# Layer 0 scan: one scan instruction for both halves of the channels, with initial states written by TensorE

## The reference

```
A = -jnp.exp(A_logs).reshape(K, d, N)            # K = 4 directions, d = 256, N = 16

def step(h, inp):
    dt_l, u_l, B_l, C_l = inp
    dA = jnp.exp(dt_l[..., None] * A)
    h = h * dA + (dt_l * u_l)[..., None] * B_l[:, :, None, :]
    y = jnp.einsum('bkdn,bkn->bkd', h, C_l)
    return (h, y)
h0 = jnp.zeros((B, K, d, N), x.dtype)            # B = 4 images
_, ys = lax.scan(step, h0, (dt_t, u_t, B_t, C_t))
```

## Time and profile before

| | us |
|---|---|
| median of 3 runs | 9207.98 (9200.64 to 9214.95) |
| profiled execution | 9207.24 |
| its span | 9205.4 |
| four passes of the scan, together | 3414.7 |

### The profile page before, as it was taken

The page is one execution under the profiler, slowest core; times in us unless marked ns, Lnnn a source line. Parts: engine busy times, 40 slices in busy tenths (PEclk is TensorE's granted clock), DMA queues, the critical chain, the costliest instruction groups (busy, mean ns, idle before and its releaser), DMA issues. The chain is left out here.

```text
span 9205.4 us, 142734 instructions
## 1 busy us (share of the span) xinstructions
PE 7794.9 (85%) x50982; PEld 6018.6 (65%) x50982; DVE 5517.8 (60%) x8186; ACT 3754.6 (41%) x7820; POOL 3974.0 (43%) x2456
## 2 busy tenths in 40 slices
PE   8999799989999899953355556688879999999999
PEld 6888588867887688841355553345656666666666
DVE  7999799979999799952233335556662222222222
ACT  6787488747876588720011112203431111111111
POOL 5888388847887488820488880031000000000000
PEclk9999999999999999975677778789999999999999
DMA  2333133312332133322455550000002222222221
GB/s 65 91 91 88 50 91 91 89 58 81 90 90 80 58 90 91 88 100 66 117 159 157 157 158 21 3 0 2 0 7 95 92 86 82 76 99 92 86 92 71
DMA packets 461971, 736.07 MB, mean 80 GB/s; under 512 B 46319, under 2 KB 366984, under 8 KB 459569
## 3 DMA queue, kind: packets, MB, share of 16 engines
q1 hardware_dynamic: 409649, 560.19, 19.4%
q0 software_dynamic: 51840, 169.91, 6.3%
HBM read 707.51 MB, written 43.72 MB: 82 GB/s over the span
## 5 line engine op out<-in xcount | busy, mean ns | idle before, releaser
L591 POOL TENSOR_TENSOR l_arena<-l_arena 128x768 f32<-128x768 f32 x1536 | 2778.6, 1824 | 470.6 <-DVE l_arena L541 408.5
L541 DVE TENSOR_TENSOR_SCAN l_arena<-l_arena,psum 128x384 f32<-128x384 f32 x3072 | 2867.9, 984 | 77.0 <-PE psum L382 41.7
L475 ACT ACTIVATE l_arena<-l_arena,l_A 128x384 f32<-128x384 f32 x3072 | 1665.3, 604 | 81.7 <-DVE l_arena L541 81.6
L384 PE MATMUL psum<-l_arena 128*128 128x128 f32 x11520 | 1579.8, 284 | 28.8 <-DVE l_arena L541 25.1
L384 PEld LDWEIGHTS psum<-l_arena 128*128 128x128 f32 x11520 | 1405.7, 192 | 185.4 <-issue 114.6
L395 PE MATMUL psum<-l_ident,l_arena 128*128 128x128 f32 x9216 | 1259.7, 273 | 53.1 <-ACT l_yT L481 45.5
L1963 DVE TENSOR_TENSOR st_Uc<-psum,st_both 128x384 f32<-128x384 f32 x512 | 285.5, 558 | 1699.8 <-PE psum L1884 1699.8
L976 POOL DMA_INDIRECT l_G<-neighbourhoods,l_idc x648 | 879.6, 1357 | 699.6 <-issue 690.4
L395 PEld LDWEIGHTS psum<-l_ident,l_arena 128*128 128x128 f32 x9216 | 1053.5, 141 | 64.3 <-POOL l_arena L591 41.5
L1884 PE MATMUL psum<-st_F,st_xt 128*128 128x384 f16 (+2 forms) x6912 | 1002.1, 290 | 0.0
L995 PE MATMUL psum<-l_ident,l_G 128*128 128x128 f32 x2592 | 450.2, 356 | 534.9 <-DVE l_G L959 534.9
(11 more groups left out here) (326 smaller groups left out, 7729.2 us busy)
## 6 DMA issues: line engine op xcount, KB each, us to landing
l_arena<-c_rows SPq DMA_DIRECT2D x1536, 192.0 KB, 3.0
st_FS<-filter_sums SPq DMA_DIRECT2D x128, 641.0 KB, 7.4
st_F<-filter_parts SPq DMA_DIRECT2D x128, 576.5 KB, 6.1
neighbourhoods<-padded_image SPq DMA_DIRECT2D x16, 1300.5 KB
st_mab<-in_st_mp SPq DMA_DIRECT2D x68, 256.0 KB, 7.4
st_mab<-in_st_mm SPq DMA_DIRECT2D x68, 256.0 KB, 7.7
l_G<-neighbourhoods,l_idc POOLq DMA_INDIRECT x648, 3.6
l_gnx<-in_x SPq DMA_DIRECT2D x4, 1152.0 KB, 5.6
```

The source lines that it names most:

```text
L384: mm = pe.matmul(ps[:, o:o + P], dtuT[:, g % 2, t, h * P:(h + 1) * P], diagB[:, rank[s] % 3, t, :], start=True, stop=True)
L475: act.activation(decay[:, s % NDC, h, :], dtv[:, g % 2, h, :], ACT.Exp, scale=A[:, g // NRC, h, n:n + 1]).then_inc(s_exp, 1)
L541: dve.tensor_tensor_scan(hbuf[:, n, h, flip], decay[:, s % NDC, h, flip], ps[:, BANK * (2 * (s % 2) + h):BANK * (2 * (s % 2) + h) + RC][:, ...
L591: pool.tensor_tensor(hC[:, s % NHC], hbuf[:, s % NS], Cs[:, s % NCS, :].unsqueeze(1).broadcast_to([P, 2, RC]), ALU.mult).then_inc(s_hc, 1)
```

## The change

`hbuf` and `decay` get rows of `RX` = 772 columns in place of 768: column 0, the 384 positions of half 0, column 385, the 384 of half 1, column 770, and one spare. The decays at columns 0, 385 and 770 are set to zero once a pass. One scan instruction goes over 770 columns, 0 to 769 forward or 770 to 1 backward, from the constant 0. Where the decay is zero the state becomes the scan's input, so TensorE writes each half's initial state into that column of PSUM: a matmul with `ident` as weights and one column of `hbuf` (or of zeros) as moving data, ahead of the half's three blocks. The PSUM set is laid so that half 0 with its column ends a bank and half 1 begins the next. `s_x2` and `s_scan` now count once a step, so waits on a half become waits on a step.

```diff
+RX = 2 * RC + 4
+X2_AT = BANK - RC - 2
...
-        hbuf = cut(0, NS * 2 * RC).rearrange("p (n h l) -> p n h l", n=NS, h=2)
+        hbuf = cut(0, NS * RX).rearrange("p (n l) -> p n l", n=NS)
...
-        decay = cut(20352, NDC * 2 * RC).rearrange("p (r h l) -> p r h l", r=NDC, h=2)
+        decay = cut(20416, NDC * RX).rearrange("p (r l) -> p r l", r=NDC)
...
+                x2_ps = [ps[:, 2 * BANK * r + X2_AT:2 * BANK * (r + 1)] for r in range(2)]
+
+                def half(h):
+
+                    return slice(1 + h * (RC + 1), 1 + h * (RC + 1) + RC)
+
+                def halves(row):
+
+                    return row[:, 1:2 * RC + 3].rearrange("p (h l) -> p h l", h=2)[:, :, 0:RC]
...
+                        if s >= 2:
+                            pe.wait_ge(s_scan, s - 1)
+                        back, first = g // NRC >= 2, g % NRC == 0
                         for h in range(2):
-                            if s >= 2:
-                                pe.wait_ge(s_scan, 2 * (s - 2) + h + 1)
+                            start, end = (half(h).stop, half(h).start) if back else (half(h).start - 1, half(h).stop - 1)
+                            o = 2 * BANK * (s % 2) + X2_AT + start
+                            pe.matmul(ps[:, o:o + 1], ident[:], decay[:, 0, 0:1] if first else hbuf[:, n, end:end + 1],
+                                      start=True, stop=True)
                             for t in range(LB):
-                                o = BANK * (2 * (s % 2) + h) + t * P
+                                o = 2 * BANK * (s % 2) + X2_AT + half(h).start + t * P
...
-                            mm.then_inc(s_x2, 1)
+                        mm.then_inc(s_x2, 1)
...
+                        if s >= NDC:
+                            act.wait_ge(s_scan, s - NDC + 1)
                         for h in range(2):
-                            if s >= NDC:
-                                act.wait_ge(s_scan, 2 * (s - NDC) + h + 1)
...
+                        run = slice(2 * RC + 2, 0, -1) if g // NRC >= 2 else slice(0, 2 * RC + 2)
                         if s >= NS:
                             dve.wait_ge(s_hc, s - NS + 1)
-                        for h in range(2):
-                            dve.wait_ge(s_exp, 2 * s + h + 1)
-                            dve.wait_ge(s_x2, 2 * s + h + 1)
-                            start = hbuf[:, n, h, last:last + 1] if j else 0.0
-                            dve.tensor_tensor_scan(hbuf[:, n, h, flip], decay[:, s % NDC, h, flip],
-                                                   ps[:, BANK * (2 * (s % 2) + h):BANK * (2 * (s % 2) + h) + RC][:, flip],
-                                                   start, ALU.mult, ALU.add).then_inc(s_scan, 1)
+                        dve.wait_ge(s_exp, 2 * s + 2)
+                        dve.wait_ge(s_x2, s + 1)
+                        dve.tensor_tensor_scan(hbuf[:, n, run], decay[:, s % NDC, run],
+                                               x2_ps[s % 2][:, run], 0.0, ALU.mult, ALU.add).then_inc(s_scan, 1)
...
+                    for end in (0, RC + 1, 2 * RC + 2):
+                        ins = dve.memset(decay[:, :, end:end + 1], 0.0)
```

More of the change, by code:

```diff
@@ L112, in layer0 @@
         sig = cut(2 * PW * PW, 2 * RC).rearrange("p (r l) -> p r l", r=2)
-        hbuf = cut(0, NS * 2 * RC).rearrange("p (n h l) -> p n h l", n=NS, h=2)
[L115 to L119, removed]
-        decay = cut(20352, NDC * 2 * RC).rearrange("p (r h l) -> p r h l", r=NDC, h=2)
-        hC = cut(23424, NHC * 2 * RC).rearrange("p (r h l) -> p r h l", r=NHC, h=2)
-        Cs = cut(26496, NCS * RC).rearrange("p (r l) -> p r l", r=NCS)
-        low = cut(28800, 2 * RC).rearrange("p (r l) -> p r l", r=2)
+        hbuf = cut(0, NS * RX).rearrange("p (n l) -> p n l", n=NS)
+        dtv, dtu = (cut(12352 + 1536 * i, 4 * RC).rearrange("p (r h l) -> p r h l", r=2, h=2) for i in range(2))
+        dtuT = cut(15424, 4 * RC).rearrange("p (r t d) -> p r t d", r=2, t=LB)
+        soft = cut(16960, 2 * RC).rearrange("p (h l) -> p h l", h=2)
+        xT = cut(17728, 4 * RC).rearrange("p (r t d) -> p r t d", r=2, t=LB)
+        diagB = cut(19264, 3 * RC).rearrange("p (r t l) -> p r t l", r=3, t=LB)
+        decay = cut(20416, NDC * RX).rearrange("p (r l) -> p r l", r=NDC)
+        hC = cut(23504, NHC * 2 * RC).rearrange("p (r h l) -> p r h l", r=NHC, h=2)
+        Cs = cut(26576, NCS * RC).rearrange("p (r l) -> p r l", r=NCS)
+        low = cut(28880, 2 * RC).rearrange("p (r l) -> p r l", r=2)
         BT = sb("BT", [P, 2, LB, NS])
@@ L462, in turned_input @@
                         if i >= 2:
-                            act.wait_ge(s_x2, 2 * turned[i - 2] + 2)
+                            act.wait_ge(s_x2, turned[i - 2] + 1)
                         for t in range(LB):
@@ L471, in decays @@
                             act.wait_ge(s_dt, 2 * g + 2)
+                        if s >= NDC:
+                            act.wait_ge(s_scan, s - NDC + 1)
                         for h in range(2):
-                            if s >= NDC:
-                                act.wait_ge(s_scan, 2 * (s - NDC) + h + 1)
-                            act.activation(decay[:, s % NDC, h, :], dtv[:, g % 2, h, :], ACT.Exp,
+                            act.activation(decay[:, s % NDC, half(h)], dtv[:, g % 2, h, :], ACT.Exp,
                                            scale=A[:, g // NRC, h, n:n + 1]).then_inc(s_exp, 1)
@@ L525, in diagonal @@
                         if i >= 3:
-                            dve.wait_ge(s_x2, 2 * straight[i - 3] + 2)
+                            dve.wait_ge(s_x2, straight[i - 3] + 1)
                         dve.tensor_tensor(diagB[:, i % 3], ident_ps.unsqueeze(1).broadcast_to([P, LB, P]),
@@ L555, in project @@
                             delta(g, 1)
+                    for end in (0, RC + 1, 2 * RC + 2):
+                        ins = dve.memset(decay[:, :, end:end + 1], 0.0)
+                    ins.then_inc(s_nil, 1)
+                    dve.wait_ge(s_nil, 1)
                     dve.wait_ge(s_id, 1)
```

11 lines of the change are left out of this document (5 added, 6 removed).

## The result

The changed kernel takes 9635.2 us (9631.0 to 9647.0, 4 runs) beside 9210.8 us (9200.6 to 9215.0, 4 runs) for the kernel before: a ratio of 1.0465, interval 1.0446 to 1.0483. It is slower, as forecast: 424 us are lost where 350 were worked out.

What follows compares the result with a forecast made beforehand. VectorE was taken as the bound, to be replaced by TensorE: 32.4 + 6.2 = 38.6 us, plus 0.8 of waits, 39.4 a chunk, 941 us a pass, +350 us in all, 9557 us. Forecast range 9400 to 9700 (0.78), wider range 9340 to 9700.

Steps and rivals of the forecast that it cites:

- The bound: In the layer 0 scan, VectorE bounds at 34.7 of 35.6 us a chunk; the change hands the bound to TensorE.
- The price of a pair: Each added f32 load and matmul pair on TensorE costs 0.107 us, half of L1318's pitch at half clock.
- the term of 6.2: TensorE's added column matmuls per chunk: 4.3 us in ten straight steps plus 1.9 in six turned ones.
- The rule of a floor per matmul: Skill's floor of 25 ns per small matmul: pairs add 1.6 us a chunk, 9115 us; cheap column, faster, chance 0.06.
- The rest of TensorE's work: TensorE's chunk without the added columns, summed from record counts times pitch plus projections: 32.4 us.
- the 32.4: TensorE's true work in us per chunk before the change, including 4.6 for the next chunk's projections.
- The 0.8 I gave to waits: TensorE's remaining waits per chunk, in us: those for ScalarE's copy or L549, and start-up at chunk borders.
- the 0.50 us before L412: First two directions: TensorE's 0.95 us wait for ScalarE's copy of the sum shrinks by 0.43, leaving 0.5.
- The merged scan: VectorE's one scan of 770 columns takes 1.79 us, 1.69 from start to start; VectorE's chunk becomes 32.8 us.
- The coarser waits: Waiting for whole scans: the loop takes 2.0 us a step against TensorE's 2.42 in straight steps, so nothing is added.
- GpSimd: Its 741 us a pass stay under 941; it matters only if a quarter slower on the shifted columns.
- The free pairs' rival: With free pairs, VectorE's 32.8 plus 0.9 idle sets 33.7 us a chunk, 9028 us; cheap column, faster, chance 0.06.

Runs made afterwards that it cites:

- no_columns: The changed kernel without its one-column matmuls, their PSUM columns zeroed once a pass and the carry between chunks left out: 9135.0 us, ratio 0.9919.
- state_through_decay: The changed kernel with initial states put into the decay row by a small ScalarE copy, no TensorE columns, one scan over 773 columns: 9149.2 us, ratio 0.9932.
- before_split: The kernel before with the rows projection in two parts and, in step 3, ScalarE's copy of the sum ahead of the projections: 9212.1 us, ratio 1.0003.
- two_scans_columns: The kernel before, two scans and waits per half kept, plus a one-column f32 matmul to an unused PSUM column ahead of each half: 9628.8 us, ratio 1.0454.

## Why the prediction was right, and by how much it was short

**The bound.** Right. VectorE's gapless chain became one with waits for L401 and L399, TensorE's idle time fell from 19.3 to 6.6 us a pass, the clock stayed at 1.00. That TensorE had about 3 us a chunk to spare (2.4 by the work as measured below), and the change asks for over 6, is what decided the sign.

**The price of a pair**, 0.107 us from L1318 at half the clock: it measured 0.22 / 2 = 0.11 us in a straight step, and a turned step lost 0.35 us, not 0.32. With 10 x 0.45 + 6 x 0.35 = 6.6 us a chunk the term of 6.2 was 0.4 us too small. Halving a pitch seen at the lower clock was sound for loads. The rule of a floor per matmul, which would have made the kernel faster, did not hold here, since each matmul brings its own load: 0.11 us a pair, not 0.025.

**The rest of TensorE's work**: this is the term that was mis-sized. A pass has 958.1 + 4.6 (the last chunk's missing projections) = 962.7 us, 40.1 a chunk for 39.4 forecast. TensorE is idle 6.6 / 24 = 0.3 us of it, so its work is 39.8, not 38.6: 0.4 is the column's price, and 0.8 is missing from the 32.4. The trace shows where: four blocks of a chunk, the L350, the L357 and both L365, use less than the whole array (128*40, 16*128, 9*128). L412 ahead of each takes 0.75 us, not 0.66, and the first column behind each takes 0.24 to 0.25, not 0.14 (488.59 to 489.87 above; L350 at 466.51 and L365 at 473.49 are alike); 4 x 0.2 = 0.8. I had summed groups by their busy times, where such a pause between groups is not seen. The 0.8 I gave to waits was really 0.3: the 0.50 us before L412 came as forecast (476.88 us in the trace, 6.1 us a pass), but only in the twelve chunks of the first two directions, and next to nothing was added to it. So the work was 1.2 us a chunk too small and the waits 0.5 too large, and that the second error hid part of the first is luck. What is left is 0.7 us a chunk, 17 us a pass, 68 us of the 74 by which the loss was undersized.

**The merged scan**: 1.79 us predicted, 1.756 measured. The Trainium skill (DVE: opcode table, instruction layouts, handler registers and perf-mode slots, § 6. Datapath and trigger behaviour) says that this instruction runs at half throughput. Twice the 0.42 us that L549 takes for 384 columns is 0.84, the pace on which the 1.79 rests, so the trace agrees to 2%. But merging is not where the gain comes from. From start to start a pair from a column takes 1.83 us (429.58 to 431.41), a pair from a constant 1.70 (101.50 to 103.20 in the same trace), and the single scan of 770 from a constant 1.68 (101.44 to 103.12 in the changed kernel's). Of the 0.15 us a step 0.13 are the constant initial state and 0.02 the merging.

**The coarser waits.** "Nothing is added" was true of this kernel but not as a property of the waits: alone they cost 83 us. I had worked out the loop for the steps in the middle of a chunk only, and there it held; it failed in the steps beside the rows projection.

**GpSimd** was to matter only if slower. Its product became faster (below).

**The free pairs' rival**, 9028 us, is nearly what no_columns tried: 9135. VectorE's work was as forecast (782.6 / 24 = 32.6 us a chunk), its idle time was not: 50.8 us of the pass, 2.1 a chunk in place of 0.9. In state_through_decay, which stands at the same pass, 1.78 us of one chunk's waits lie before the scan of step 1 (419.15 above). TensorE's real work of 32.4 + 0.8 = 33.2 us lies above VectorE's 32.8, with one step of buffer between them, and each long block then shows. That the near balance and the one-step buffer are the cause is argued from the releasers, not shown by a run: a third PSUM set was not tried.

## What to carry to other kernels

A one-column matmul costs its weight loads, and uncovers its neighbour's: count load and matmul pairs (two for f32), here about 0.11 us each, before moving a tiny write to the engine with the least spare time. Small per-step values can often ride on an operand that another engine writes anyway, as the initial state does here in the decay row. When an engine is freed, look for the next wait by place within the chunk and not by averages, and test order edits apart: a gain and a loss of the same size hid each other in before_split.

## What the runs showed of the hardware

- A change between matmuls of the whole array and of fewer columns or rows cost about 0.1 us in and 0.1 out (L350, L357 and L365 in the changed kernel), and the load behind it starts with its matmul, not 0.11 us ahead; 128x32 weights between 128x128 ones made a column 0.35 us where the whole array's took 0.22, though the load was shorter (108 for 191 ns).
- In the earlier trace rows a pair of scans from a constant is 0.12 us shorter than a pair from a column; one scan of 770 from a constant takes 1.756 us, against 1.91 for the pair.
- GpSimd's product of 768 columns took 1824 ns in the kernel before (L591) and in two_scans_columns 1823, but 1686 in the changed kernel (L608) and 1680 to 1687 in all with a merged scan. The number of columns is the same. VectorE's scan beside it is not the cause: the last product of a pass runs when all scans are done, and it takes 1.80 us in the kernel before (at 952.34) and 1.81 in two_scans_columns (1058.02), but 1.68 in the changed kernel (1060.36) and in no_columns (934.07). That leaves the layout of the product's input, whose halves are now one column apart and begin at an odd column; no run changed it alone.
- The matmul L350 with strided moving data needed 2.7 us for four records of 384 columns (466.51 to 469.19), 0.67 each; L365, not strided, took 0.84 for two, 0.42 each.
